# Taking a context chunk's layer-norm statistics two chunks ahead, and turning every chunk from the second projection on

## The reference, cut to what matters

```python
# x: 8 x 1024 x 512, context: 8 x 2048 x 512, 16 heads of 32
xn = layer_norm(layernorm(x), g1, b1)       # two norms, one after the other
cn = layer_norm(context, g2, b2)
q, k, v = xn @ Wq.T, cn @ Wk.T, cn @ Wv.T
scores = q @ k.T / sqrt(32)                 # masked
x = x + softmax(scores) @ v @ Wo.T + bo
x = x + quantised(layernorm(x)) @ quantised(W).T + bias     # blocks of 32 to a 6 bit grid
```

## Time and profile before

| | us |
|---|---|
| median of 3 runs (lowest, highest) | 4893.51 (4892.85, 4898.69) |
| the profiled execution | 4894.66 |
| its span, from the first instruction to the last | 4892.9 |

### The profile page before, as it was taken

One profiled execution on the slowest core, in us unless ns is written; L12 is line 12 of the kernel. 1 busy time (PEld: TensorE's weight loads), 2 busy tenths in 40 slices (PEclk: granted clock), 3 DMA queues, 4 the chain that ended last, 5 costly groups with the idle time before them and its releaser, 6 DMA issues.

```text
span 4892.9 us, 65384 instructions
## 1 busy us (share of the span) xinstructions
PE 4593.8 (94%) x24720; PEld 1348.4 (28%) x24720; DVE 3379.8 (69%) x3943; ACT 2838.0 (58%) x5128; POOL 2971.8 (61%) x1818
## 2 busy tenths in 40 slices
PE   4999899998999989999899998999989999899998
PEld 2322242222422224222242222422224222342222
DVE  4788457884588855888357884588855887458873
ACT  3477634775347753477544774457744577446773
POOL 2278743777438773387634876347863578625875
PEclk9999999999999999999999999999999999999999
DMA  5255632555325553355533555335543355443552
GB/s 182 64 118 104 147 113 60 118 111 152 99 65 105 119 147 102 70 104 118 141 102 71 111 110 140 104 72 117 108 134 109 73 116 112 127 113 80 106 119 75
DMA packets 189918, 530.81 MB, mean 108 GB/s; under 512 B 28625, under 2 KB 102673, under 8 KB 148386
## 3 DMA queue, kind: packets, MB, share of 16 engines
q0 software_dynamic: 43776, 318.79, 32.3%
q1 hardware_dynamic: 145826, 207.83, 13.8%
HBM read 110.98 MB, written 21.01 MB: 27 GB/s over the span
## 4 chain that ended last, share of the span: by engine, by line
PE 75%; ACT 10%; DVE 6%; SPq 3%; DMA 3%; issue 2%; POOL 1%; ACTq 0%; DVEq 0%; POOLq 0%
PE banks L957 21%; PE banks L947 19%; PE banks L864 12%; PE banks L923 9%; PE banks L858 7%; ACT region L743 7%; PE banks L983 5%; DVE max_parts L583 3%; SPq L293 3%; PE banks L833 2%; DMA region<-in_x 1%; DVE region L574 1%; ACT values L814 1%; ACT region L718 0%; POOL wkT_wvT_wqT L399 0%
## 5 line engine op out<-in xcount | busy, mean ns | idle before, releaser
L583 DVE TENSOR_REDUCE max_parts<-banks 128x2 f32<-128x1024 f32 x2048 | 2400.1, 1218 | 469.2 <-PE banks L923 468.2
L743 ACT ACTIVATE region<-banks 128x512 f32<-128x512 f32 x4096 | 2211.0, 596 | 695.9 <-PE banks L947 656.9
L399 POOL TENSOR_TENSOR wkT_wvT_wqT<-region 128x1024 f32<-128x1024 f32 x608 | 1474.7, 2549 | 556.5 <-ACT region L743 554.3
L947 PE MATMUL banks<-queries_stacked,keys_stacked 98*128 98x512 f16 x4096 | 1298.4, 387 | 82.2 <-ACT region L743 50.7
L957 PE MATMUL banks<-region,values 128*32 128x512 f32 x8192 | 1100.6, 609 | 18.5 <-ACT region L743 7.7
L947 PEld LDWEIGHTS banks<-queries_stacked,keys_stacked 98*128 98x128 f16 x4096 | 289.0, 97 | 1438.7 <-ACT region L743 1356.4
L923 PE MATMUL banks<-keys_stacked,queries_stacked 33*128 33x512 f16 x4096 | 658.7, 384 | 7.0 <-DVE max_parts L583 3.5
L864 PE MATMUL banks<-region,wkT_wvT_wqT 128*128 128x512 f16 x2304 | 574.6, 388 | 48.1 <-POOL region L380 23.0
L601 DVE RECIPROCAL row_sums_inverse<-row_sums_inverse 128x128 f32<-128x128 f32 x256 | 232.0, 930 | 437.9 <-ACT row_sums_inverse L760 437.9
L399 POOL TENSOR_TENSOR sums<-region 128x1024 f32<-128x1024 f32 x160 | 395.7, 2631 | 25.7 <-ACT region L743 25.5
L574 DVE SCALAR_TENSOR_TENSOR region<-banks,region 128x512 f16<-128x512 f32 x192 | 132.2, 689 | 346.7 <-ACT region L726 345.7
(11 more groups left out here) (83 smaller groups left out, 2905.3 us busy)
## 6 DMA issues: line engine op xcount, KB each, us to landing
wdT<-wkT_wvT_wqT POOLq DMA_DIRECT2D x96, 1024.0 KB, 11.4
wkT_wvT_wqT<-wkT_wvT_wqT POOLq DMA_DIRECT2D x80, 1024.0 KB, 7.0
sums<-wkT_wvT_wqT POOLq DMA_DIRECT2D x72, 1024.0 KB, 7.0
keys_stacked<-region SPq DMA_DIRECT2D x768, 64.0 KB, 2.0
wkT_wvT_wqT<-sums POOLq DMA_DIRECT2D x40, 1024.0 KB, 7.0
region<-in_x SPq DMA_DIRECT2D x24, 1024.0 KB, 10.0
wkT_wvT_wqT<-weights_split SPq DMA_DIRECT2D x8, 3072.0 KB, 19.3
queries_stacked<-region SPq DMA_DIRECT2D x384, 64.0 KB, 2.0
```

Of the source, the lines that this page charges most:

```text
L399: e.tensor_tensor(SUMS[dst][:, half], PR[i][:, half], PR[i + 1][:, half], ALU.add).then_inc(s_pr, 1)
L583: e.tensor_reduce(mpart[:, buf, :, a, t, c], MXB[parity], AX.X, ALU.max).then_inc(s_mxd, 1)
L743: e.activation(PR[u % 4][:, j * HALF:j * HALF + HALF], score_bank(kt, j)[0], ACT.Exp, scale=SCALE).then_inc(s_ex, 1)
L947: e.matmul(dst, KA[0:STR, ds(ka + (j * C + (u + 1) * P), P)], QA[0:STR, ds(qa[j], HALF)], start=True, stop=True).then_inc(s_st, 1)
```

## The change

For every context chunk c, the statistics move in DVE's list from (c - 1, 0) to (c - 2, 2), behind the low part of (c - 2, 1) and ahead of that of (c - 2, 2). The centring stands at (c - 1, 0) for all. Chunks 2 and 3 are turned in the second and third projection of the chunk before them, as chunks 1, 4 and 5 were already. ACT's list follows that. SP's and POOL's lists stay as they were, as do all instructions and their number.

```diff
-    turn_at = lambda f: 2 if f in (XCH - 1, XCH) else 1
+    TURN_AT = 1
...
                 done = 0
+                parts = iter(())
                 for j, (p, f, i) in enumerate(FRONT):
                     if j > 0 and FRONT[j - 1][0] == "qk":
                         low_part(*FRONT[j - 1][1:])
+
                     if p == "qk" and i == 0:
+                        next(parts, None)
+                    if p == "qk" and i == 2:
                         parts = iter(())
-                        if XCH <= f + 1 < NCH:
-                            parts = norm(f + 1, b, b * CALLS + (CALLS_FIRST + f + 2 - XCH))
-                        if turn_at(f) == 1:
-                            next(parts, None)
-                    if p == "qk":
+                        if f + 2 < NCH:
+                            parts = norm(f + 2, b, b * CALLS + (CALLS_FIRST + f + 3 - XCH))
                         next(parts, None)
...
-                        if 0 <= i + 1 - turn_at(f) < 2 and f + 1 < NCH:
+                        if 0 <= i + 1 - TURN_AT < 2 and f + 1 < NCH:
...
-                        if p == "qk" and i == turn_at(f) and f + 1 < NCH:
+                        if p == "qk" and i == TURN_AT and f + 1 < NCH:
                             turns = turn_chunk(b, f + 1)
-                        turning = turns if p == "qk" and i - turn_at(f) in (0, 1) and f + 1 < NCH else iter(())
+                        turning = turns if p == "qk" and i - TURN_AT in (0, 1) and f + 1 < NCH else iter(())
```

More of the change, by code:

```diff
@@ L792, in _ @@
                         high_part(f, i, j)
-                        if 0 <= i + 1 - turn_at(f) < 2 and f + 1 < NCH:
-                            if f == 0 and i + 1 == turn_at(f):
+                        if 0 <= i + 1 - TURN_AT < 2 and f + 1 < NCH:
+                            if f == 0 and i + 1 == TURN_AT:
                                 e.wait_ge(s_out[1], b * 64 + 16)
-                            turned(b, f + 1, (f + 1) % 2, int(f + 1 < XCH), range(CC // 2 * (i + 1 - turn_at(f)), CC // 2 * (i + 2 - turn_at(f))))
+                            turned(b, f + 1, (f + 1) % 2, int(f + 1 < XCH), range(CC // 2 * (i + 1 - TURN_AT), CC // 2 * (i + 2 - TURN_AT)))
                     else:
```

## The result

The changed kernel took 4974.4 us (four runs, 4968.9 to 4977.8), the kernel before beside it 4894.4. The ratio is 1.0161, with a 95% interval from 1.0143 to 1.0179: 80 us slower. The forecast was 4979, range 4952 to 4994.

What follows compares the result with a forecast made beforehand. PE is busy 94% of the span, but SP's issues set the pace early in each front. Late loads cost 72.4 us over eight batches, the clock 12; added to 4894.66 this gave 4979 us, range 4952 to 4994.

Steps and rivals of the forecast that it cites:

- The first wait: At (1, 2), DVE's statistics of chunk 3 wait for their load; (2, 0) starts 4.5 us later.
- The feedback through SP: The late low part of (1, 3) delays SP's second 12 issues of stack(1); chunk 4's load issues at 714.4, not 711.80.
- The sum of the path: Issue of chunk 3's load (T3) to v(2, 0): 29.37 us against 20.04 in the second batch; 72.4 us over eight.
- Nothing is given back: From v(2, 0) to (4, 0) PE has no idle time to absorb the delay; the head starts later by all of it.
- The clock: After PE's wait before v(2, 0), TensorE's slower clock costs 1.5 us a batch, 12 us in all; bounds 0 and 1.8.
- the row of a wait of 2.57 us: Kernel before, PE ahead of (2, 0): the 27 matmuls behind this wait took 7.69 us for 5.9, losing 1.8.
- Small terms: Chunk 2's statistics make PE's (1, 0) some 1.3 us late at no cost; chunk 5's cost 0 to 0.2 us.
- The signs: Expected in timelines: DVE waits some 6 us for each load; PE idles 7 to 8 before (2, 0), 3 to 5 before v(2, 0).
- the gain of 3.2 us a batch: At (2, 0): with DVE free and chunk 2 turned earlier, PE would start at 698.24 instead of 701.42.
- rival 1: Chunk 3's load lands in time, so (2, 0) starts at 698.24: 26 us gained, 4869 us; chance 4%.
- the prediction's first part: Ahead of (2, 0) SP sets the pace, not PE: 24 gapless issues take 15.40 us, the next 24 15.67.

Runs made afterwards that it cites:

- chunk 3 alone: The kernel before with only chunk 3's statistics moved early, to (1, 2); 4923.1 us, ratio 1.0059.
- the filler: The changed kernel plus matmuls nobody reads in PE's waits, 38 ahead of (2, 0) and 24 ahead of v(2, 0); 4964.7 us.
- Chunk 4 alone: The kernel before with only chunk 4's statistics moved early, to (2, 2); 4968.2 us, ratio 1.0153.
- run with the load first: The changed kernel with each context chunk's load issued ahead of SP's 24 issues for the chunk three before it; 4895.2 us.
- the one with the load between: The changed kernel with each context chunk's load issued between the two twelves of SP's issues for the chunk three before it; 4901.2 us.

## Why the prediction was right, point by point

**The first wait.** Forecast: the statistics of chunk 3 wait for a load that lands 6.5 us after its issue, and the low part of (1, 2) behind them releases (2, 0). Measured 6.77 us to the statistics' start, and (2, 0) 10.7 us after the issue (718.36 - 707.66) for 10.5. Right.

**The feedback through SP.** Forecast 19.0 us between the loads of chunks 3 and 4; the eight fronts have 19.0 in the mean (16.5 before). Right, and chunk 3 alone shows the same without the second wait, 19.1.

**The sum of the path.** Forecast 29.37 us from T3 to v(2, 0); the mean is 29.21, from 28.5 to 30.4. The growth is 8.9 us a batch, 71 in eight, for 72.4.

**Nothing is given back.** The fronts, (0, 0) to the first maximum, grew by 10.7 us each, 86 in all; the span grew by 79. Most of the other 7 us lie spread over the seven stretches between a first maximum and the next front, 524.4 us in the mean before and 523.8 now. Over all profiles these lie between 522.6 and 524.8 with no relation to the edits, and chunk 3 alone, where the fronts grew by 40 us and the time by 27, has the 522.6. Whether something is given back there or the executions just differ stays open. Without it the time would have been 2 us above the forecast; with it, it is 5 below.

**The clock.** Forecast 1.5 us a batch, 12 in all, between bounds of 0 and 1.8. The profile of the changed kernel has 1.5 more a batch for v(2)'s matmuls, and the filler took 10.5 us off the time. The step was right, and the row of a wait of 2.57 us with a loss behind it was the one to go by. Chunk 4 alone, with 7.1 us of wait before v(2, 0), lost 2.4 a batch, so the upper bound of 1.8 was too low as a bound.

**Small terms.** Chunk 2's statistics cost PE 0.98 us before (1, 0), forecast 1.3, and T3 did not move (24.3 us after (0, 0) in the mean, as before). Chunk 5's cost 0.16 us, forecast 0 to 0.2.

**The signs.** DVE's two waits were to be some 6 us each and are 8.57 and 4.59; PE's before (2, 0) was to be 7 to 8 us and is 9.23, as PE came to it earlier, 25.5 us after (0, 0) for 27.1. These sizes do not enter the sum, which goes from the load's issue on. The range's lower end was worked out as 4954 and then given as 4952, without a reason for the 2 us.

**Where the prediction was wrong** is in a part that did not decide the time: the gain of 3.2 us a batch for a DVE that is free, and with it rival 1's 26 us. I followed it to (2, 0) and no further. v(2, 0) needs the low part of (2, 2), its high part before that, and this needs the second half of stack(1), whose last issue ends at 711.8 before. The high part of (1, 2) came 1.45 us after the end of stack(0)'s last issue (695.41 to 696.86), the low part 0.63 later and PE 0.75 after that the earlier trace rows; the same for (2, 2) makes 714.6, only 0.9 us ahead of where v(2, 0) stands now. SP's 48 issues would have kept all but that of the 3.2. The run with the load first showed this, and the one with the load between again. That SP and not PE sets the pace there stood in the prediction's first part; I used it for the loss and not for the gain. The change's purpose was sound, but two things had to be moved with it.

## What to carry to other kernels

Before an instruction is moved ahead in an engine's list, look at when its data land, not at when its engine is free: the wait comes with it and holds up all that stands behind. Then look at what issues that load. Here it stood behind 24 DMAs on one queue that themselves waited for the engine now blocked, so that the first wait made the next load late too. And follow a gain to the next two meeting points before it is counted; a queue without gaps in its issues is a bound like an engine at full work. A load in time only undid the loss of 80 us here; the gain came when a quarter of the issues went to another engine's queue as well (57 us, 4901 to 4844). In the kernel before, both together gave nothing.

## What the runs showed of the hardware

- A 64 KB DMA took SP's queue 0.64 to 0.67 us where it issued without a gap (24 in 15.4 to 16.0 us in the rows above, 18 in 11.8). On ACT's queue three took 1.9 to 2.2 us in the second batch, and 3.1 in one place, with ACT's next activation behind them; others ran beside ACT's own activations.
- After a wait of PE of 4.4 us the next 3.5 us had the clock at 0.59 (between 1.2 and 2.4 GHz, mostly the lower). With waits of 7.0 to 8.1 us (chunk 4 alone) v(2)'s 48 matmuls took 12.9 us in the mean for 10.5. Near 3 us it went either way: in one of the changed kernel's eight batches, after 2.98 us, they took 10.53, and in two batches of its run with the load first, after 2.71 us, 12.22.
- A load of 256 KB landed in 2.8 to 3.0 us (medians) beside the same small DMAs, one of 1 MB in 6.0 to 6.5.
